# Layer norm, decayed linear attention and a routed feed-forward on one core: first half of x transposed in two chunks of tokens, keys of both feature halves by chunk, two clearings and part of the end reordered

## What is computed

```python
xn = layernorm(x)                                  # per token, eps 1e-5
# attention: 16 heads of 16 features
q, k, v = split(xn @ w_qkv)                        # 256 -> 3 x 256
q, k = elu(q) + 1, elu(k) + 1
kv   = scan over tokens: s = decay * s + k * v     # decay = sigmoid(decay_param), one per head
ksum = scan over tokens: s = decay * s + k
att  = (q * kv / clip(sum_in_head(q * ksum), 1e-6)) @ w_out
# feed-forward: one expert of eight per token, and a shared one
logits = xn @ router_w.T ; expert = argmax ; gate = sigmoid(max)
routed = (silu(g) * u) @ w_down[expert], g, u = split((gate * xn) @ w_gate_up[expert])
shared = (silu(g) * u) @ shared_down,    g, u = split(xn @ shared_gate_up)
out = x + att + routed + shared
```

## Time and profile before

| | us |
|---|---|
| median of 3 runs | 131.84 (131.7 to 132.1) |
| the profiled execution | 131.59 |
| its span, first to last instruction | 130.0 |
| PE busy | 124.3 (96% of the span) |
| DVE busy | 80.4 (62%) |
| ACT busy | 51.8 (40%) |
| POOL busy | 33.3 (26%) |

### The profile page before, as it was taken

One profiled execution on the slowest core, in us unless ns is written; L12 is line 12 of the kernel. 1 busy time (PEld: TensorE's weight loads), 2 busy tenths in 40 slices (PEclk: granted clock), 3 DMA queues, 4 the chain that ended last, 5 costly groups with the idle time before them and its releaser, 6 DMA issues.

```text
span 130.0 us, 2419 instructions
## 1 busy us (share of the span) xinstructions
PE 124.3 (96%) x835; PEld 107.6 (83%) x835; DVE 80.4 (62%) x167; ACT 51.8 (40%) x103; POOL 33.3 (26%) x56
## 2 busy tenths in 40 slices
PE   4989999999999999999999999999999999999990
PEld 1257767787888588999999999999999968999980
DVE  0899886999999968865575553515030447922191
ACT  1565796979955645321222222242222237200000
POOL 7914000007988100020202020202020202687500
PEclk9999999999999999999999999999999999999999
DMA  2673999999982200158798879898881121033445
GB/s 98 218 252 86 342 342 215 185 269 386 402 323 92 64 26 3 42 112 321 233 289 284 327 238 294 275 304 257 299 273 53 27 72 48 11 95 96 124 140 185
DMA packets 15588, 25.02 MB, mean 193 GB/s; under 512 B 1260, under 2 KB 12436, under 8 KB 15576
## 3 DMA queue, kind: packets, MB, share of 16 engines
q1 hardware_dynamic: 13896, 21.17, 51.7%
q0 software_dynamic: 1344, 3.43, 8.8%
q10 hardware_dynamic: 336, 0.27, 0.6%
HBM read 18.78 MB, written 6.08 MB: 191 GB/s over the span
## 4 chain that ended last, share of the span: by engine, by line
PE 93%; DVE 2%; issue 1%; POOL 1%; ACT 0%; DVEq 0%; POOLq 0%
PE ps L1092 24%; PE ps L1106 12%; PE ps L290 10%; PE ps L291 9%; PE ps L292 9%; PE ps L950 5%; PE ps L956 4%; PE ps L963 4%; PE ps L1036 4%; PE ps L1030 3%; PE ps L1022 2%; PE ps L896 1%; DVE x_sb L872 1%; DVE x_sb L867 1%; PE ps L1003 1%
## 5 line engine op out<-in xcount | busy, mean ns | idle before, releaser
L1092 PE MATMUL ps<-xgT,gu 128*128 128x144 f32 x256 | 34.1, 287 | 0.0
L1092 PEld LDWEIGHTS ps<-xgT,gu 128*128 128x128 f32 x256 | 32.3, 190 | 0.2 <-ACT xgT L518 0.2
L803 DVE TENSOR_TENSOR wqkv<-rz,ps 128x288 f32<-128x288 f32 x16 | 7.3, 454 | 26.2 <-ACT rz L554 26.1
L425 POOL DMA_DIRECT2D sorted_rows<-yrow x9 | 6.3, 697 | 59.8 <-DVE yrow L798 59.8
L1106 PE MATMUL ps<-wqkv,dn 128*128 128x144 f32 x128 | 17.4, 289 | 0.0
L554 ACT ACTIVATE rz<-ps 128x288 f32<-128x288 f32 x16 | 6.6, 411 | 26.8 <-PE ps L1092 26.8
L1106 PEld LDWEIGHTS ps<-wqkv,dn 128*128 128x128 f32 x128 | 16.1, 190 | 0.0
L417 POOL DMA_INDIRECT sorted_rows<-xn,slot_row x8 | 11.2, 1398 | 19.2 <-ACT xn L490 17.3
L290 PE MATMUL ps<-xT_hi,sgu_hi 128*128 128x512 f32 x32 | 13.1, 408 | 0.0
L292 PE MATMUL ps<-xT_hi,sgu_lo 128*128 128x512 f32 x32 | 12.5, 391 | 0.0
L291 PE MATMUL ps<-xT_lo,sgu_hi 128*128 128x512 f32 x32 | 12.5, 390 | 0.0
(11 more groups left out here) (158 smaller groups left out, 225.1 us busy)
## 6 DMA issues: line engine op xcount, KB each, us to landing
gu<-in_L_ffn_w_gate_up_dram SPq DMA_DIRECT2D x8, 1024.0 KB
dn<-in_L_ffn_w_down_dram SPq DMA_DIRECT2D x8, 512.0 KB
sorted_rows<-zeros SPq DMA_DIRECT2D x1, 2592.0 KB, 17.7
wqkv<-sorted_rows SPq DMA_DIRECT2D x10, 144.0 KB
sorted_rows<-yrow POOLq DMA_DIRECT2D x9, 144.0 KB, 3.0
sgu<-_ffn_shared_gate_up_dram SPq DMA_DIRECT2D x1, 1024.0 KB, 6.0
out_dram<-x_sb SPq DMA_DIRECT2D x8, 128.0 KB, 1.8
wqkv<-in_L_attn_w_qkv_dram SPq DMA_DIRECT2D x3, 256.0 KB, 3.5
```

The source lines that it names most:

```text
L803: V.tensor_tensor(hr[:, 2 * h:2 * h + 2, :].rearrange("p f s -> p (f s)"), act_sb[:, h, 0:2 * SLOTS], ps[:, 2 * h + 1, 0:2 * SLOTS], ALU.m ...
L1092: ins = mm(ps[:, 2 * h + u, (f % 2) * SLOTS:(f % 2 + 1) * SLOTS], gu[p][:, kc, col:col + P], xgT[:, kc, :], start=(kc == 0), stop=(kc == K ...
```

## The change

- The first 512 tokens are transposed in two chunks of 256 (`transpose_chunk`), the first into banks 4 and 5, the second into 6 and 7. ACT rounds and DVE subtracts one chunk at a time, both feature halves in one instruction. The order of the normalised tiles changes with it: ACT takes tile 1, DVE tiles 0, 2, 3 (and ACT tile 7, DVE 4, 5, 6 as before). The router's transposed weights move to bank 2, since bank 7 is now used.
- `key_chunk(h)` computes the keys of both feature halves for one chunk, tile 0 in bank 0 and tile 3 in bank 3, with 12 matmuls of 256 columns for each chunk. So tile 3 is done ahead of tiles 1 and 2, and behind the transposes of the second half comes tile 4. A wait for `s_rlo` stands ahead of tile 1, since tile 2 overwrites bank 2.
- On DVE the statistics of tiles 4 and 5 move behind the two subtractions of x.
- POOL clears `yT` and `yrow` behind the rest of the query weights.
- At the end all four spreads stand together ahead of shared tile (7, 0), the last result is transposed back into bank 6, DVE adds all eight gathered tiles ahead of the eight PSUM sums, and the output tiles go out in turn from ACT's queue (even ones) and SP's (odd ones).

```diff
@@ constants
+        CH = 256
+        def qkv_done(t):
+            return {1: 3, 2: 4, 3: 2}.get(t, t + 1)
-        spread_bank = [0, 1, 4, 5]
+        spread_bank = [0, 1, 4, 7]
+        LAST_BACK = 6
@@ SP
-            for i in range(NT):
+            for i in range(1, NT, 2):
                 sp.wait_ge(s_fin, i + 1)
                 sp.dma_start(out_rows[:, i, :], x_sb[:, i, :]).then_inc(s_out, 16)
@@ ACT
-                for i in range(n * TH + 3, (n + 1) * TH):
+                for i in ((1,), (NT - 1,))[n]:
...
+            def x_hi_chunk(h):
+                act.wait_ge(s_xT, h + 1)
+                A(xT_hi[:, :, h * CH:(h + 1) * CH], ps[:, 4 + h * KC:4 + (h + 1) * KC, 0:CH], ACT.Copy).then_inc(s_xhi, 1)
...
             norm(0)
+            x_hi_chunk(0)
+            x_hi_chunk(1)
             act.wait_ge(s_rT, 1)
-            A(rT[:, :, 0, :], ps[:, 7, 0:KC * E].rearrange("p (c e) -> p c e", e=E), ACT.Copy).then_inc(s_rhi, 1)
-
-            x_hi(0)
+            A(rT[:, :, 0, :], ps[:, 2, 0:KC * E].rearrange("p (c e) -> p c e", e=E), ACT.Copy).then_inc(s_rhi, 1)
...
+            for i in range(0, NT, 2):
+                act.wait_ge(s_fin, i + 1)
+                act.dma_start(out_rows[:, i, :], x_sb[:, i, :]).then_inc(s_out, 16)
@@ DVE
-                for i in range(n * TH, n * TH + 3):
+                for i in ((0, 2, 3), (4, 5, 6))[n]:
...
+            def x_lo_chunk(h):
+                cols = slice(h * CH, (h + 1) * CH)
+                dve.wait_ge(s_xhi, h + 1)
+                V.tensor_tensor(xT_lo[:, :, cols], ps[:, 4 + h * KC:4 + (h + 1) * KC, 0:CH], xT_hi[:, :, cols].bitcast(F32), ALU.subtract).then_inc(s_xlo, 1)
...
             w_lo(1).then_inc(s_wlk, 1)
+            x_lo_chunk(0)
+            x_lo_chunk(1)
             for i in range(TH, TH + 2):
                 statistics(i)
-            x_lo(0)
...
-            for i in range(TH + 1):
+            for i in range(NT):
                 rows_add(i)
             for i in range(NT):
                 dense_add(i)
-                if 0 < i < TH:
-                    rows_add(i + TH)
@@ PE
+            def transpose_chunk(h):
+                for j in range(2):
+                    if (h, j) == (0, 1):
+                        pe.wait_ge(s_xna, 1)
+                    else:
+                        pe.wait_ge(s_xn, 2 + j if h else 1)
+                    for c in range(KC):
+                        ins = tr(ps[:, 4 + h * KC + c, j * P:(j + 1) * P], xn[:, 2 * h + j, c * P:(c + 1) * P], ident[:, :])
+                ins.then_inc(s_xT, 1)
...
+            def key_chunk(h):
+                rows = slice(h * CH, (h + 1) * CH)
+                pe.wait_ge(s_whk, 1)
+                pe.wait_ge(s_xhi, h + 1)
+                for c in range(KC):
+                    for kc in range(KC):
+                        mm(ps[:, 3 * c, rows], wqkv_hi[:, kc, D + c * P:D + (c + 1) * P], xT_hi[:, kc, rows], start=(kc == 0), stop=False)
+                pe.wait_ge(s_wlk, 1)
...
+                pe.wait_ge(s_xlo, h + 1)
+                for c in range(KC):
+                    for kc in range(KC):
+                        ins = mm(ps[:, 3 * c, rows], wqkv_hi[:, kc, D + c * P:D + (c + 1) * P], xT_lo[:, kc, rows], start=False, stop=(kc == KC - 1))
+                    if h:
+                        ins.then_inc(s_qkv, 1)
...
-            transpose_tokens(0)
-            for t in range(3):
-                qkv_tile(t)
+            transpose_chunk(0)
+            transpose_chunk(1)
+            key_chunk(0)
+            key_chunk(1)
+            pe.wait_ge(s_rlo, 1)
+            qkv_tile(1)
+            qkv_tile(2)
             router_logits(0)
-            transpose_tokens(1)
-            qkv_tile(3)
+            transpose_half()
+            qkv_tile(4)
             router_logits(1)
...
-            qkv_tile(4)
+            qkv_tile(5)
             transpose_logits()
-            qkv_tile(5)
             qkv_tile(6)
             ranks()
...
-            spread_reciprocals(range(NH * KC - 1))
+            pe.wait_ge(s_yrow, total + 1)
+            spread_reciprocals()
             shared_tile(LAST, 0)
-            spread_reciprocals([NH * KC - 1])
             shared_tile(LAST, 1)
```

More of the change, by code:

```diff
@@ L393, in _ @@
             pool.memset(ones8[:, :], 1.0).then_inc(s_const, 1)
-            pool.memset(yT[:, :, :], 0.0).then_inc(s_yT, 1)
-            pool.memset(yrow[:, :, :, :], 0.0).then_inc(s_yrow, 1)
             pool.wait_ge(s_const, 15)
@@ L410, in _ @@
             pool.tensor_tensor(wqkv_lo[:, :, 0:D], wqkv[:, :, 0:D], wqkv_hi[:, :, 0:D].bitcast(F32), ALU.subtract).then_inc(s_wlq, 1)
+            pool.memset(yT[:, :, :], 0.0).then_inc(s_yT, 1)
+            pool.memset(yrow[:, :, :, :], 0.0).then_inc(s_yrow, 1)
             pool.wait_ge(s_zero, 16)
@@ L482, in _ @@
             norm(1)
-            x_hi(1)
+            x_hi_half()
             def scale_tokens(tiles):
@@ L1006, in head_sums, with spread_reciprocals @@
                 tr(ps[:, HROW, 0:P], head_of[:, :, :].rearrange("p b h -> p (b h)"), ident[:, :]).then_inc(s_hrow, 1)
-            def spread_reciprocals(gs):
+            def spread_reciprocals():
                 pe.wait_ge(s_rsplit, 1)
                 pe.wait_ge(s_hrowc, 1)
-                for g in gs:
+                for g in range(NH * KC):
                     rows = slice(g * STRIP, g * STRIP + 2 * HC)
```

78 lines of the change are left out of this document (33 added, 45 removed).

## The result

| | before | after |
|---|---|---|
| median, us | 131.73 (131.42 to 132.1, 8 executions) | 137.32 (134.24 to 138.92, 8 executions) |
| the profiled execution, us | 131.59 | 138.92 |
| its span, us | 130.0 | 137.3 |
| its mean granted clock | 1.0 | 0.973 |

Slower by 5.6 us in the median, and the executions of the changed kernel differ by 4.7 us among themselves. One thing has to be known to read this: they differ by the clock that PE was granted. Two at a mean of 1.0 took 134.24 and 134.8, two at 0.987 took 136.06 and 136.87, and four at 0.975 to 0.950 took 137.78 to 138.92. The ratio of 1.0252 (1.022 to 1.0285) leaves out the five executions that are more than 1.5% above the fastest, and of the three that are left (134.24, 134.8 and 136.06) the last had a clock of 0.987.

The account below looks back on a forecast made before the run. PE was taken to bound the kernel (93% of the chain, clock full). Profiled 131.59 + 3.6 (front and stalls) + 0 (end) = 135.2, 135.4 us for the median; forecast 134.7 to 136.4 (chance 0.70), range 133.8 to 137.2.

Parts of the forecast that it names:

- What bounds the kernel: PE holds 93% of the chain that ended last, clock full; other engines matter only where PE waits.
- the first stall: PE ready at 16.23 behind the second half's transposes, idle 3.0 us until DVE's key sum; tile 4 starts at 19.2.
- The second stall: Ahead of tile 7, PE waits 1.0 us for the second key sum; tile 7 at 27.0, 3.4 us later.
- the shift: Delay carried from the stalls through DVE to the sums per head and experts: 3.6 us, between 3.2 and 4.1.
- The front: Chunked transposes and keys: first product at 8.87 instead of 9.15, second half's transposes done earlier, 0.6 us gain at most.
- The clearings: POOL's moved clearings collide with DVE's second eps addition at about 12.5; counted 0, up to 0.5 us if cover fails.
- The end: Spreads together, gathered tiles added first, two output queues: worth -0.4 to +0.3 us, taken as 0.
- rival 2: PE's clock falls to 1.2 GHz after its 3.0 us idle, slowing tiles 4 to 7: 0 to 5 us, middle 137.9; chance 0.10.
- Rival 1: Stalls ahead of tiles 4 and 7 real but shorter: +1 to +2.9, 132.8 to 134.7 us; chance 0.12.
- Rival 3: Delay absorbed if weight transfers set the experts' stage: faster, 131.4 us; chance 0.04.
- Rival 4: Change takes less of PE's cover than thought, tile 4 starting on other grounds: no difference; chance 0.04.

Follow-up runs that it names:

- experiment 2: Kernel before with only PE's tile order of the changed kernel (tiles 0, 3, 1, 2, then 4 behind the transposes): 137.27 us, ratio 1.0373.
- experiment 3: Changed kernel with tile 0's relu and exp ahead of ACT's rounding of the second half and its key sum early on DVE: 132.39 us, ratio 1.0084.
- experiment 1: Changed kernel with eleven products on constants between the second half's transposes and tile 4, filling PE's idle time: 134.39 us, ratio 1.0226.
- experiment 4: Changed kernel with only tile 0's keys by chunk, tile 3 back behind the second half's transposes, tile 4 where it was: 131.93 us, ratio 1.0012.
- experiment 11: Kernel of experiment 5 with the two clearings back at the start of GpSimd's list: 130.86 us, ratio 0.9951.
- experiment 7: Kernel of experiment 1 with the two clearings back at the start of GpSimd's list: 134.49 us, ratio 1.0218.
- experiment 5: Kernel of experiment 4 with the statistics of tiles 4 and 5 back ahead of the two subtractions of x: 131.30 us, ratio 0.9957.
- experiment 6: Kernel of experiment 3 with the statistics of tiles 4 and 5 back ahead of the subtractions of x: 132.21 us, ratio 1.0017.
- experiment 8: Kernel before with only the changed kernel's end (spreads, last result's bank, order of sums, two output queues): 131.07 us, ratio 0.9969.
- experiment 10: Kernel of experiment 8 with both queues, but DVE adds gathered rows and PSUM in turn as before: 130.89 us, ratio 0.9953.
- experiment 9: Kernel of experiment 8 with all eight outputs issued by SP: 131.67 us, ratio 1.0007.

## Why the prediction was right and wrong

**What bounds the kernel, and the first stall: right.** PE idle until DVE's key sum, at the place named. I had PE ready at 16.23 and tile 4 at 19.2; by starts it was 15.80 + 0.79 = 16.59 and 19.54, a stall of 2.95 against 3.0. Experiment 2 shows that the order alone makes it, and experiment 3 that it hangs on the chain of rounding, relu, exp and key sum.

**The second stall and the shift: right in size.** Free of the clock (experiment 1, whose PE starts its transposes 0.15 us earlier than before, at 7.43): tile 6 would be done at 24.51 + 1.50 = 26.01, tile 7 starts at 27.07, 1.06 against the 1.0 of the text. Tile 7 is 3.51 later than in the earlier trace rows; I had 3.4. The shift that reaches the experts is 54.60 - 50.91 = 3.69 (first rounding of the sorted tokens on ACT), and 108.77 - 105.17 = 3.60 is left at DVE's first sum of spread values. The text had 3.6.

**The front: wrong, and small.** I had the first product at 8.87; it starts at 9.14, as before (9.15). The failed step is the sum 7.58 + 0.40 + 0.1 = 8.1 for ACT's first rounding, which started at 8.40. It has two errors. PE began its transposes at 7.71 in this execution, since its products on constants lasted 5.80 us instead of 5.66. And the 0.40 counts the starts of four transposes only; the last of them itself takes 0.27 us (8.09 to 8.36), so rounding follows the first transpose by 0.69, not by 0.5. In experiments 4 and 11, where PE begins at 7.58, rounding starts at 8.27 and 8.28 and the first product at 9.01 and 9.02: a chunk gives 0.14 us here, not 0.3. Before, the signal came behind four transposes too, and the fourth started at 8.04, behind DVE's last normalised tile (7.99). What the chunks did give is that the 24 key products run without a wait (2.93 us, I had 2.85): 12.07 + 3.73 + 0.79 = 16.59, 0.23 ahead of 16.82. That is what became of the 0.6 "at most" of the text.

**The clearings: right at 0** (experiment 7). In after the clearings hold it less than I feared: the first addition took 0.17 us and the second 0.34, from 12.76 to 13.10. It ended 0.02 behind the clearing of `yT` (12.74 to 13.08), and that of `yrow` (13.02 to 13.99) did not hold it. So the collision that the text called sure came, but with the smaller clearing only. Experiment 5 shows the bad case, 1.23 us through both.

**The statistics: a part that I didn't price.** I moved them in one half-sentence. Their place decides whether DVE's or GpSimd's subtraction of weights is first, and up to 1 us of time in executions where PE has no other wait (experiments 3 to 6).

**The end: the value was off, and lies at the edge of my range or past it.** I took 0 from -0.4 to +0.3; experiment 8 gives -0.5 by the medians (131.07 against 131.58) and -0.4 by the ratio (its interval is 0.9944 to 0.9994). The mis-sized step is the last gather. I had it land at 124.7 or 0.2 later and the last gathered tile added at 124.9; it was added at 123.51. The issues on GpSimd came closer together and the last one started at 120.79 against 121.21, and it landed 2.7 us later instead of 3.5 (in both profiles it is the only one of the eight whose landing is in the trace). It is 3.3 to 3.9 in the three profiles with the old order of sums (before, experiments 2 and 10) and 2.7 to 2.8 in the others that have it; why isn't shown. With the last gathered tile added early, DVE's last sum waits for PE, and PE's own end and the two queues count.

**The sum with the clock up.** 131.59 + 3.60 - 0.74 (the last sum of experiment 1 ends at 130.20, which is 2.86 later than 127.34, of the 3.60) = 134.45, and the execution took 134.34. The forecast of 135.4 is 1.0 above this: 0.7 by the end, the rest by the median of before that I added. So 134.24 and 134.8, the executions of after with the clock up, lie below and at the lower end of the forecast (134.7 to 136.4), with the stalls as I had them. That the ratio of 1.0252 gives 135.05 us, nearer to 135.4, is in part luck: one of its three executions has a slow stretch.

**The clock: the mechanism named, its chance wrong.** The median of 137.32 lies 0.1 above the upper end of my range and is rival 2, to which I gave 0.10. It came true in six of eight executions. The text described it rightly: PE busy before, then 3.0 us idle, "the tiles from 4 to 7 take up to twice as long", between 0 and 5 us, middle 137.9. The profiled execution lost 3.4 us of PE's full speed to it, and tile 7 came 2.98 us later by it. What was wrong is the chance. The only ground that the text gives is that no row of before showed a fall; but no row of before showed PE idle that long either, which I had written one sentence earlier. A row that can't contain the case says nothing against it. In hindsight an even chance and a range up to about 139 would have been fair.

**Rival 1** (shorter stalls) is refuted by the rows above; that 134.24 and experiment 1's 134.39 lie in its 132.8 to 134.7 is the end's doing, not that of shorter stalls. **Rival 3** (absorption) is refuted too: of the shift of 3.69 at the start of the experts 3.60 is left 54 us later. **Rival 4** is refuted by experiment 2.

## What to carry to other kernels

Before work is moved forward on an engine that runs its list in order, look up what the moved work had been covering: here a tile, the router's logits and the decay's products, 3.0 us together, stood between the transposes and a bank whose user ends 2.8 us later, and the new order opened two waits for 0.2 us gained. When a change opens an idle stretch on TensorE longer than any in the profile, price the lower clock as a likely outcome, not as a remote one (here 11 of 14 executions of the two kernels whose profiles show 2.71 us of idle time), and look at the spread of executions; filling the stretch with products on constants is a quick way to tell the two losses apart. Two subtractions on VectorE and GpSimd that started within 0.1 to 0.3 us of each other were a coin toss of about 1 us here, and a harmless-looking swap ahead of them had set it up.

## What the runs showed of the hardware beyond what I expected

- **The same wait brings the clock down at different moments and for different times.** In the profile of after PE restarts at 19.54, the clock is 1.00 up to 20 us, 0.86 in the next us, then 0.50 until 27. In that of experiment 2 it is down already when PE restarts at 19.71 (0.72 in 19 to 20, the two products take 1.19 us), and up again at 23. The two kernels whose profiles show 2.71 us idle had a fall in 6 of 8 and 5 of 6 executions. The kernel with 0.97 us in its profile had none in 12, and those with the stretch filled (0.33 us left, experiments 1 and 7) none in 12. The Trainium skill ("TensorE: Matmul & The Clock Gate", section "HAM oscillation — how this bites in real kernels") tells of kernels whose waits put the array back to half rate; here the traces agree, with the difference that the same wait doesn't do it every time, nor for the same length.
- **A pause of PE without a releaser.** Every profile with the new end has one among PE's last 144 products, between the 118th and the 121st: 0.45 us in experiment 8, 0.59 in 11, 0.47 in 9, 0.33 in 10, 0.34 in 1 and 0.21 in after. The two with the old end (before and experiment 2) have none. It is not tied to how many products ran ahead of it (experiment 1 has eleven more and the same place), nor to the order of sums or the queues (experiments 9 and 10). What it is stays open; without it the new end could be worth up to about 0.4 us more, an estimate from the 0.45 of experiment 8.
- **A clearing on GpSimd can hold a four-column addition on DVE** until it ends: 1.23 us in experiment 5, 0.84 in the earlier trace rows and 0.34 in after, against 0.17 without it. In experiment 5 it was held through two clearings, in after by the first alone; what decides that isn't shown.
